# The adapter of a four-layer kernel: each batch's own columns by transfer, narrow fp32 products and one stacked product

## The reference, cut to what matters

```
x = x + L0(x)   # 64x64 weight chosen per batch (200 of them)
x = x + L1(x)   # attention over a paged cache, window 256, 8 heads, new keys and values written to the pages
x = x + L2(x)   # expert: x @ W[id] + b[id], 16 experts of 512x512
x = x + L3(x)   # x @ W.T + scalings[a] * ((x @ A[a].T) @ Bm[a].T), a = adapter number of the batch
```

## Time and profile before

| | us |
|---|---|
| median of 3 runs | 1035.92 |
| lowest and highest | 1035.61, 1037.2 |
| the profiled execution | 1039.95 |
| its span, first to last instruction | 1038.1 |
| PE busy in the span | 999.5 (96%) |
| DVE busy | 660.5 (64%) |
| POOL busy | 542.8 (52%) |
| ACT busy | 537.7 (52%) |

### The profile page before, as it was taken

The page is one execution under the profiler, slowest core; times in us unless marked ns, Lnnn a source line. Parts: engine busy times, 40 slices in busy tenths (PEclk is TensorE's granted clock), DMA queues, the critical chain, the costliest instruction groups (busy, mean ns, idle before and its releaser), DMA issues.

```text
span 1038.1 us, 24050 instructions
## 1 busy us (share of the span) xinstructions
PE 999.5 (96%) x6438; PEld 714.4 (69%) x6438; DVE 660.5 (64%) x1928; ACT 537.7 (52%) x1337; POOL 542.8 (52%) x597
## 2 busy tenths in 40 slices
PE   8998999999768999999999999999999999999998
PEld 6676777767635777766777766677766677777666
DVE  5897898666744656556656556655655665565562
ACT  4347776667444544455445455554545545544551
POOL 3553644446675555556555555656645555555500
PEclk9999999999969999999999999999999999999999
DMA  4333453365447767777677777767777776777650
GB/s 142 115 126 125 137 171 126 104 201 190 148 123 224 211 194 240 229 205 245 205 215 228 219 202 224 219 196 232 223 213 197 233 210 205 216 237 205 201 201 21
DMA packets 95338, 196.17 MB, mean 189 GB/s; under 512 B 31346, under 2 KB 40114, under 8 KB 87110
## 3 DMA queue, kind: packets, MB, share of 16 engines
q1 hardware_dynamic: 63942, 149.49, 45.8%
q0 software_dynamic: 30784, 44.16, 15.5%
q10 hardware_dynamic: 576, 2.10, 0.6%
HBM read 195.08 MB, written 33.56 MB: 220 GB/s over the span
## 4 chain that ended last, share of the span: by engine, by line
PE 68%; issue 1%; POOL 1%; DMA 1%; DVE 0%; ACT 0%; POOLq 0%; SPq 0%; DVEq 0%; ACTq 0%
PE bank L93 15%; PE bank L1506 12%; PE bank L1460 9%; PE bank L1481 9%; PE bank L1468 8%; PE bank L1556 6%; PE bank L1436 4%; PE bank L1447 3%; PE bank L1560 3%; DMA W<-in_w 1%; POOL KV L1152 0%; DMA KVE<-in_pool,idxs_e 0%; POOL KVE L1162 0%; POOL KV L1162 0%; PE bank L1527 0%
## 5 line engine op out<-in xcount | busy, mean ns | idle before, releaser
L1266 ACT ACTIVATE PR<-SM,nb 128x336 f32<-128x336 f32 x256 | 147.5, 585 | 6.5 <-DVE nb L1338 6.3
L1162 POOL DMA_INDIRECT KV<-kv_scratch,idxs x96 | 96.6, 1007 | 101.0 <-DMA KV<-in_pool,idxs 77.0
L1162 POOL DMA_INDIRECT KVE<-kv_scratch,idxs_e x93 | 93.4, 1004 | 95.6 <-DMA KVE<-in_pool,idxs_e 71.0
L1257 ACT ACTIVATE PT<-bank 112x384 f32<-112x384 f32 x256 | 111.4, 489 | 56.1 <-PE bank L1468 55.1
L1506 PE MATMUL bank<-W,XT 128*64 128x512 f32 x512 | 126.2, 609 | 3.7 <-DMA W<-in_w 3.7
L1152 POOL DMA_INDIRECT KV<-in_pool,idxs x96 | 98.8, 1029 | 49.2 <-issue 24.8
L1152 POOL DMA_INDIRECT KVE<-in_pool,idxs_e x90 | 92.9, 1032 | 54.5 <-issue 30.0
L93 PE MATMUL bank<-wqh,XTH 128*128 128x512 f32 x256 | 106.5, 416 | 9.0 <-DVE XTL L506 6.0
L1468 PE MATMUL bank<-ident,PR 128*112 128x128 f32 x768 | 108.8, 278 | 2.6 <-DVE PR L1345 2.6
L1468 PEld LDWEIGHTS bank<-ident,PR 128*112 128x112 f32 x768 | 83.5, 134 | 34.4 <-DVE PR L1345 19.8
L93 PE MATMUL bank<-wql,XTH 128*128 128x512 f32 x256 | 101.8, 398 | 0.0
(11 more groups left out here) (204 smaller groups left out, 2338.0 us busy)
## 6 DMA issues: line engine op xcount, KB each, us to landing
W<-in_w SPq DMA_DIRECT2D x64, 1024.0 KB, 5.6
X<-in_x SPq DMA_DIRECT2D x32, 256.0 KB, 2.9
x_scratch<-X SPq DMA_DIRECT2D x32, 256.0 KB, 2.0
qt_scratch<-QT SPq DMA_DIRECT2D x32, 256.0 KB, 2.9
XB<-x_scratch SPq DMA_DIRECT2D x32, 256.0 KB
BB<-in_b SPq DMA_DIRECT2D x64, 128.0 KB
out_dram<-XO SPq DMA_DIRECT2D x32, 256.0 KB
kv_scratch<-KVR SPq DMA_DIRECT2D x31, 256.0 KB, 3.1
```

The lines of the kernel that those rows point to most:

```text
L1162: pool.indirect_dma_start(out=KV[k][:, c, :], out_offset=None, in_=kv_d, in_offset=bass.IndirectOffsetOnAxis(ap=idxs[k][:, NCH + c:NCH + c ...
L1257: return nc.scalar.activation(dst, src, ACT.Copy)
L1266: nc.scalar.activation(PR[u % 2][:, :], SM[u % 2][:, :], ACT.Exp, bias=nb[:, u:u + 1], scale=SCALE, accum_out=rs[:, u:u + 1]).then_inc(s_e, 1)
```

## The change

The adapter no longer multiplies by all 8 adapters and masks. SP fetches for each batch its own part by its number:

- `AS` (SBUF, made in the first stage by ACT) holds each adapter's columns of A four times over, so 4 x 16 = 64 columns per 128 features. Two DMAs a pair copy 128 KB each from `AS` to `AG`.
- `bs_scratch` (DRAM, stored in the first stage by 4 DMAs, 1 MB in all) holds for each adapter 64 rows: high, high, low, low part of the scaled B. Two DMAs a pair copy 64 rows of 512 each (128 KB) to `BG`.
- `adapter` is 8 fp32 products (16 PE instructions): stationary 128 x 64 of `AG`, moving 64 columns of x3 turned, the two batches in the two column halves of the array, into 64 columns of bank 7.
- DVE makes from it `XA`, two 64 x 64 blocks on a diagonal whose rows are high, low, high, low part, and `adapted_sum` is one fp32r pass of 512 columns, `XA` by `BG`.
- ACT now copies the turned x3 whole to `XT3` (fp32). DVE makes both `XTH3` (a copy) and `XTL3` from it, in the place where `XTL3` was made.
- On PE `adapted_sum` stands in the middle of `output`, after two of its four column groups; `adapter` waits for the whole x3 and the A transfers, `dense3_low` for the low part.
- SP issues the four transfers between the store and `weights(1)`.
- In the first stage the late weights are four parts, not five; added are the scaling of B on DVE, two copies on ACT (2048 and 512 columns), a subtraction of 512 columns on DVE and the store of B.

```diff
+        bs_d = nc.dram_tensor("bs_scratch", [NA, 4, RANK, D], F32).ap()
...
+            BSH, BSL = (trig[:, :, :, :].rearrange("p a b c -> p (a b c)")[:, i * D:(i + 1) * D].bitcast(F32R)
+                        for i in range(2))
...
                 def late_low(i):
                     def run():
-                        dve.wait_ge(s_wlh, i + 1)
+                        dve.wait_ge(s_wlh, i + 1 + i // 2)
                         part = slice(i * 1024, (i + 1) * 1024)
                         split(wlh[:, part], wll[:, part], wlr[:, part]).then_inc(s_wl, 1)
                     return run
+
+                def scale_b():
+                    dve.wait_ge(s_wlate, 16 * 6)
+                    v.tensor_scalar(b_raw, b_raw, scal[:, 0:1], None, ALU.mult).then_inc(s_bsc, 1)
+
+                def adapter_low():
+                    dve.wait_ge(s_wlh, 3)
+                    split(BSH, BSL, b_raw).then_inc(s_wl, 1)
...
-                between.update({27: late_low(0), 28: late_low(1), 29: late_low(2),
-                                31: in_turn(late_low(3), late_low(4))})
+                between.update({21: go_on(1), 23: go_on(2), 26: in_turn(go_on(4), scale_b)})
+                between.update({27: late_low(0), 28: late_low(1), 29: adapter_low, 30: late_low(2), 31: late_low(3)})
...
+                def store_b():
+                    sp.wait_ge(s_wl, 3)
+                    for g in range(4):
+                        sp.dma_start(bs_d[:, g], (BSH, BSL)[g // 2].bitcast(F32)).then_inc(s_bso, 16)
...
+                    30: store_b,
...
+                def adapter_high():
+                    act.wait_ge(s_bsc, 1)
+                    copy(AS[:, :, :, :], a_raw.rearrange("p (e r) -> p e r", r=RANK).unsqueeze(2).to_broadcast(
+                        [P, NA * KC, 4, RANK]))
+                    copy(BSH, b_raw).then_inc(s_wlh, 1)
...
+                       {26: in_turn(late_high(0), late_high(1)), 27: adapter_high, 28: late_high(2), 29: late_high(3)})
...
+                    def adapter_columns(q):
+                        numbers = [sp.value_load(aid[0:1, bass.ds(q * 2 + b, 1)], min_val=0, max_val=NA - 1)
+                                   for b in range(2)]
+                        wait(sp, s_xa, q)
+                        for b, e in enumerate(numbers):
+                            sp.dma_start(AG[:, b, :], AS[:, :, :, :].rearrange("p (e k) s r -> p e (k s r)", e=NA)
+                                         [:, bass.ds(e, 1)].rearrange("p o c -> p (o c)")).then_inc(s_ag, 16)
+                        wait(sp, s_l3, q)
+                        for b, e in enumerate(numbers):
+                            sp.dma_start(BG[b * T:(b + 1) * T, :].bitcast(F32), bs_d[bass.ds(e, 1)]
+                                         .rearrange("o g r n -> (o g r) n")).then_inc(s_bg, 16)
...
                         store(pr.move(-2))
+                    if dense:
+                        adapter_columns(p - 1)
...
-                        copy(XTH3[:, :, :].rearrange("p k t -> p (k t)"), bank[7][:, :]).then_inc(s_xt3h, 1)
+                        copy(XT3[:, :, :].rearrange("p k t -> p (k t)"), bank[7][:, :]).then_inc(s_xt3f, 1)
...
+                        dve.wait_ge(s_xt3f, at(r, 1, 0))
+                        wait(dve, s_l3, r)
+                        v.tensor_copy(XTH3[:, :, :], XT3[:, :, :]).then_inc(s_xt3h, 1)
                         dve.wait_ge(s_xt3h, at(r, 1, 0))
-                        low(XTL3[:, :, :].rearrange("p k t -> p (k t)"), bank[7][:, :],
-                            XTH3[:, :, :].rearrange("p k t -> p (k t)")).then_inc(s_xt3, 1)
+                        low(XTL3[:, :, :], XT3[:, :, :], XTH3[:, :, :]).then_inc(s_xt3, 1)
...
-                        v.tensor_tensor(XAM[:, :, :], bank[1 if last_dense(p) else 7][:, 0:P].rearrange("p (b t) -> p b t", b=2),
-                                        adapt[:, bass.ds(r * 2, 2)].unsqueeze(2).to_broadcast([P, 2, T]),
-                                        ALU.mult).then_inc(s_xam, 1)
-                        xam = XAM[:, :, :].rearrange("p b t -> p (b t)")
+                        xa = bank[1 if last_dense(p) else 7][:, 0:T]
+                        v.tensor_copy(XAH[:, :], xa).then_inc(s_xah, 1)
+                        v.tensor_scalar(XAM[:, :], xa, sel[:, 1:2], None, ALU.mult).then_inc(s_xam, 1)
+                        dve.wait_ge(s_xah, at(r, 1, 0))
                         dve.wait_ge(s_xam, at(r, 1, 0))
-                        v.tensor_copy(XAH[:, :], xam).then_inc(s_xah, 1)
-                        dve.wait_ge(s_xah, at(r, 1, 0))
-                        low(XAL[:, :], xam, XAH[:, :]).then_inc(s_xal, 1)
+                        wait(dve, s_l3, r)
+                        for b in range(2):
+                            rows = slice(b * T, (b + 1) * T)
+                            v.scalar_tensor_tensor(XA[rows, rows], XAH[rows, :].bitcast(F32), sel[rows, 0:1],
+                                                   XAM[rows, :], ALU.mult, ALU.add).then_inc(s_xal, 1)
...
                 def adapter(r, of):
-                    pe.wait_ge(s_xt3, at(r, 1, 0))
-                    exact_products(mm, bank[of][:, 0:P], [(a_h[:, k, :], a_l[:, k, :], *x3t[k]) for k in range(KC)],
-                                   True, True).then_inc(s_xa, 1)
+                    pe.wait_ge(s_xt3f, at(r, 1, 0))
+                    pe.wait_ge(s_ag, at(r, 32, 31))
+                    for k in range(KC):
+                        for b in range(2):
+                            rows = slice(b * T, (b + 1) * T)
+                            last = mm(bank[of][rows, 0:T], AG[:, b, k * T:(k + 1) * T], XT3[:, k, rows],
+                                      start=k == 0, stop=k == KC - 1, skip_group_check=True)
+                    last.then_inc(s_xa, 1)
 
                 def adapted_sum(r, of):
-                    pe.wait_ge(s_xal, at(r, 1, 0))
-                    exact_products(mm, bank[of][:, :], [(XAH[:, :], XAL[:, :], b_h[:, 0, :], b_l[:, 0, :])],
-                                   False, True).then_inc(s_l3, 1)
+                    pe.wait_ge(s_xal, at(r, 2, 1))
+                    pe.wait_ge(s_bg, at(r, 32, 31))
+                    mm(bank[of][:, :], XA[:, :], BG[:, :], start=False, stop=True).then_inc(s_l3, 1)
...
-                def dense3_low():
+                def dense3_low(r):
+                    pe.wait_ge(s_xt3, at(r, 1, 0))
                     for k in range(KC):
                         mm(bank[6][:, :], XTL3[:, k, :], w3_h[:, k, :], start=False, stop=False)
...
-                        dense3_low()
+                        dense3_low(r)
+                    if dense:
+                        if adapted:
+                            pe.wait_ge(s_xah, at(r, 1, 0))
+                            pe.wait_ge(s_xam, at(r, 1, 0))
+                        output(q, 0, 2)
+                    if adapted:
                         adapted_sum(r, 6)
                     if dense:
-                        if adapted:
-                            pe.wait_ge(s_xam, at(r, 1, 0))
-                        output(q, 0, KC)
+                        output(q, 2, KC)
                     if attention:
```

More of the change, by code:

```diff
@@ L129, in build @@
         eid = sb("eid", [1, NB], I32)
[L130 removed]
+        aid = sb("aid", [1, NB], I32)
+        sel = sb("sel", [P, 2])
         KVE = sb("KVE", [CH, 2 * NCH * KVW])
@@ L137, in build @@
         FM_e = [early[:, D + i * SPAN:D + (i + 1) * SPAN] for i in range(2)]
-        NWL = KC * D * 2 + KC * P + D
+        NWL = KC * D * 2
+        NWR = NWL + KC * P + D
         wlh = sb("wlh", [P, NWL], F32R)
         wll = sb("wll", [P, NWL], F32R)
+        AS = sb("AS", [P, NA * KC, 4, RANK])
         def late(tile, which):
-            a, n = {"wo": (0, D), "w3": (KC * D, D), "a": (2 * KC * D, P), "b": (2 * KC * D + KC * P, D)}[which]
-            k = 1 if which == "b" else KC
-            return tile[:, a:a + k * n].rearrange("p (k n) -> p k n", k=k)
+            a = {"wo": 0, "w3": KC * D}[which]
+            return tile[:, a:a + KC * D].rearrange("p (k n) -> p k n", k=KC)
         s_const = sem("const_ready")
@@ L173, in build @@
         s_wl = sem("late_split")
+        s_bsc = sem("b_scaled")
+        s_bso = sem("b_stored")
         s_xth = sem("x1t_high")
@@ L211, in sa @@
                 return pa.enter_context(nc.sbuf_tensor(name, shape, dt))
-            wlr = sa("wlr", [P, NWL])
+            wlr = sa("wlr", [P, NWR])
+            a_raw = wlr[:, NWL:NWL + KC * P]
+            b_raw = wlr[:, NWL + KC * P:NWR]
             wqkv = wlr[:, 0:KC * 1024].rearrange("p (k n) -> p k n", k=KC)
@@ L484, in indices @@
                     yield
-                    step(v.tensor_scalar(pns[:, :], pni[:, :], 4, None, ALU.arith_shift_right))
+                    step(v.tensor_scalar(pns[:, :], pni[:, :], 4, 1, ALU.arith_shift_right, ALU.bitwise_and))
                     yield
@@ L489, in indices @@
                     yield
```

(23 more changed lines are left out.)

15 lines of the change are left out of this document (7 added, 8 removed).

## The result

The changed kernel takes 1088.93 us, the median of 4 runs (1083.62 to 1092.73), against 1036.56 (1035.61 to 1040.33) for the kernel before: ratio 1.0494, 95% interval [1.0442, 1.0547]. It is slower by 52 us where 9 less were forecast, and outside the range. The profiled execution took 1087.78 us, with a span of 1086.0; before it was 1038.1.

A forecast was written before the change was run, and what follows sets the result against it. PE was taken as the bound, end to end over a pair of 22.53 us. Pairs -6.3, ends -2.2, boundary -0.6 and early A +0.5 gave -8.6 us: median 1027.3, range 1018 to 1042.

The forecast's parts named there:

- What leaves PE: On PE, adapter with values shrinks by 0.65 us and the stacked product by 0.46: 1.11 us a pair.
- rivals 1 and 3: Narrow adapter products on PE: at 0.055 us each, 1035.0 us (chance 0.18); at 0.075, 1045 us (chance 0.07).
- the values behind would speed up: On PE, the values behind the new adapter in column halves would take 0.66 us instead of 0.81.
- The stacked product: `adapted_sum` on PE as one pass in place of three: 0.46 us a pair leave.
- What enters before `dense3_high`: PE waits there for DVE's copy to `XTH3`, 0.42 us long: 0.90 us a pair, bounds 0.75 and 1.16.
- rival 2: POOL's gathers hold up DVE's copy, middle price 0.5 us a pair: 1042 us, chance 0.10.
- Rival 6: The wait before `dense3_high` does not show because DVE comes earlier: 1000 us, chance 0.03.
- Ends and boundary: Bodies 32 and 33 gain 2.2 us together; the boundary after the last pair gains 0.6, bounds 0 and 1.2.
- an early A: In the first bodies the transfers have a shorter lead: 0.5 us booked once, bounds 0 and 5.
- Transfers: Four DMAs a pair, 0.5 MB, hidden in the middle; POOL could take 2.2 us more in every other pair: nothing.
- Rival 5: Fuller DMA makes the gathers the bound and the pair stays at 22.5 us: about 1034 us, chance 0.07.
- rival 4: A lands late for PE, 1 us in each pair: 1057 us, chance 0.05.

The follow-up runs named there:

- g2: Changed kernel with the four transfers made for the first pair only, later pairs reusing that A and B: 1032.41 us, ratio 0.9958 to the kernel before.
- g4: Changed kernel with the four transfers issued ahead of `weights(0)` and x3's high part made by ACT again: 1047.68 us, ratio 1.0119 to the kernel before.
- g1: Changed kernel with the four transfers issued ahead of `weights(0)`: 1049.46 us, ratio 1.0126 to the kernel before.
- g3: Changed kernel with each pair's transfers in the late place but into unread tiles, products using A and B fetched once: 1082.55 us, ratio 1.0441.
- h3: g2 with each pair's two number loads kept in SP's list: 1132.71 us, in a job where the kernel before took 1120.66.
- i2: Changed kernel without per-pair transfers, ACT copying A and B by number and making x3's high part: 1114.14 us, kernel before 1125.53 there.
- f1: Changed kernel with the four transfers issued ahead of `weights(0)`: 1113.78 us, in a job where the kernel before took 1161.79.
- h1: Kernel before plus two number loads and the four transfers per pair into unread tiles: 1097.21 us, kernel before 1120.66 there.

## Why the prediction was wrong, step by step

**What leaves PE: right.** The timeline of PE's loads before, and then in g2:

```profile
720.77 0.35 PEld L1447 LDWEIGHTS bank<-ident,KV 112*128 112x128 f32 x3
...
722.59 0.19 PEld L1556 LDWEIGHTS bank<-wll,XTH 128*128 128x128 f32 x1
...
725.23 0.30 PEld L1460 LDWEIGHTS bank<-KT,QB 64*128 64x128 f32 x4 [0.17 <-issue]
```

```profile
704.23 0.19 PEld L1579 LDWEIGHTS bank<-BG,XA 128*128 128x128 f32 x1
704.47 0.19 PEld L93 LDWEIGHTS bank<-wlh,OTH 128*128 128x128 f32 x1
...
717.98 0.35 PEld L1499 LDWEIGHTS bank<-ident,KV 112*128 112x128 f32 x3
719.19 0.19 PEld L1614 LDWEIGHTS bank<-wlh,XTH 128*128 128x128 f32 x1 [0.87 <-DVE XTH L1421]
...
720.70 0.19 PEld L1614 LDWEIGHTS bank<-wll,XTH 128*128 128x128 f32 x1
721.25 0.55 PEld L1572 LDWEIGHTS bank<-XT,AG 128*64 128x64 f32 x16 [0.37 <-issue]
721.71 0.64 PEld L1533 LDWEIGHTS bank<-PT,KVE 112*64 112x64 f32 x12
722.52 0.30 PEld L1512 LDWEIGHTS bank<-KT,QB 64*128 64x128 f32 x4 [0.17 <-issue]
```

From the last load of `dense3_high` to the scores' first load it was 725.23 - 722.59 = 2.64 us before and is 722.52 - 720.70 = 1.82 now: 0.82 leave for 0.65 forecast, and so in each of the 27 pairs from 400 to 1000 us. The sixteen narrow instructions start 0.029 us apart (0.46 / 16), near the floor of 0.0275, so rivals 1 and 3 fall. The first of them comes 0.55 us behind the last load of `dense3_high` (720.70 to 721.25); the old adapter's came 0.23 behind. That the values behind would speed up did not hold (0.81 as before), which the adapter's pace makes good: the sum was nearly right with two terms off against each other. The Trainium skill (TensorE: Matmul & The Clock Gate, LDWEIGHTS) would have 53 ns for each load of 64 columns; in two column halves they did not add up in series. The halves take turns, so each has a load every 0.058 us, which agrees. The stacked product takes 0.24 for 0.70 (three loads 0.23 apart): 0.46, as forecast.

**What enters before `dense3_high`: right in place and kind, too small by 0.2.** The start of L1614 lies 1.21 us behind that of L1499's transposes; before, L1556's (721.08) lay 0.31 behind L1447's: 0.90. That is the least: in every other pair it is 0.3 more (the copy starts later on DVE), and over 400 to 1000 us the mean is 1.08 us more than before, for 0.90 forecast. So the 1.28 that leave and the 1.08 that enter are both 0.2 above the forecast's 1.11 and 0.90, and that their difference comes out near is in part luck. Most of g2's pairs alternate between 22.17 and 22.47, mean of all 22.41, for 22.32 forecast. In the changed kernel the same wait stands (701.65 to 702.13), and the copy takes (the line's view, then one case):

```profile
L1421 DVE CAST XTH<-XT x32: 417/427/642, 336.8 to 1077.8; 128x512 fp32r<-128x512 f32 x32
```

```profile
701.65 0.43 DVE L1421 CAST XTH<-XT 128x512 fp32r<-128x512 f32 x1
...
702.13 0.19 PEld L1614 LDWEIGHTS bank<-wlh,XTH 128*128 128x128 f32 x1 [0.87 <-DVE XTH L1421]
```

427 ns in the middle, 642 at most, for 0.42 forecast. No copy was held for a gather's 1 us, so rival 2 falls by its size. It is not nothing: six of the 32 copies took 0.47 to 0.64 us, each with a gather under way, like the one at 724.16 (0.63 us) beside the gather at 723.58 shown above; together 0.7 us in the whole run. Other copies of the same kernel were as short as ever inside a gather's record (383.37, 0.43 us, in the gather from 383.00 to 383.99). So the rule of the exclusive lock (the Trainium skill, SBUF: State Buffer, "SBUF: two separate sides") is borne out only in part, with no full gather of waiting. That the copy in its turn holds up gathers can't be the loss either, since g2 has the same 32 copies. Rival 6 falls by the same wait.

**Ends and boundary: right.** g2's span of 1030.7 is 7.4 below before: pairs 4.1 (forecast 6.1 for 29), start 0.6 (0.6), the last body and the end 2.75 (2.2). The forecast without its 0.5 for an early A is 9.1 for this. By the medians of one job it is only 4.9, since the profiled execution of before was 4.0 above the median; so the work on PE gave half to four fifths of what was forecast for it.

**Transfers: wrong, and the whole of the miss.** Two sentences failed. "8 to 8.5. That is hidden": behind the two number loads A is issued 2.75 us after `weights(0)` (720.97 - 718.22), not directly, and `weights(0)` itself comes later when the gathers do, as it waits for them. And the one that carries the loss: "POOL could take that much more before it set the pace: nothing." The slack was read rightly as far as it went (KVE's 24.5 us; KV has 23.5 more, and both are 1.8 us a pair), but its user was not sized. By POOL's clock over 400 to 1000 us, divided by the number of pairs in them (600 over the mean distance):

| kernel | mean pair | landing waits | waits for PE | the rest |
|---|---|---|---|---|
| before | 22.55 | 4.7 | 1.8 | 16.0 |
| g2, no transfers | 22.41 | 5.7 | 0.9 | 15.8 |
| g4, early, ACT high | 22.70 | 7.0 | 0 | 15.7 |
| g1, early | 23.00 | 7.3 | 0 | 15.7 |
| g3, late, unread | 24.14 | 8.7 | 0 | 15.5 |
| after | 24.25 | 8.8 | 0 | 15.5 |

The rest is the twelve gathers at 1.3 us each, which no run shortened. So POOL's loop is 15.5 to 16 us plus the landings, and before it had 1.8 us left. From before to after, the landing waits grew by 4.1 us. Less the slack that is 2.3, and less the 0.5 by which the rest is smaller, it is, but for rounding, the 1.7 by which a pair grew. This is bookkeeping; what the transfers did is g3 against g2, which differ by them and by what SP does for them (number loads and waits): landing waits 3.0 longer, 0.9 of that taken from the waits for PE and 0.3 from the rest, and a pair of 24.14 for 22.41, 1.73 more or 50 us in 29 pairs. (The other 1.0 of the 4.1 is in g2 too.) The trace of before had a place to see it, though it is not in the rows above the prediction: the half in which the four transfers go out was the one with the quick landing, 2.1 us; A and B are issued beside its gathers. The error was to ask only whether A is in time, and not what A delays. Rival 5 named the mechanism, with a chance of 0.07, but kept the pair at 22.5, as if the gathers could only use up the gain; rival 4 had the price, by a wait that g3 shows not to be the cause.

**Still open.** How much of the 3.0 is bytes and how much SP's time: h3 was made for that, and its condition spoiled it. For bytes speak two things. SP itself idles for landed gathers for 283.6 us in the changed kernel between 290 and 1050 us, so its 1.8 us for numbers are mostly covered. And in the code POOL's gathers wait for PE, for POOL's own copies and for landings, never for SP, so SP's time can lengthen POOL's loop only through when its transfers meet the gathers. That is argued, not shown by a run. Why the same bytes cost 33 us more in the late place than in the early one: the table has it as landings, 8.7 for 7.3 us a pair, but which transfer stood in front of which gather there was not separated. And whether the adapter without transfers beats the kernel before with the selection made: g2 shows that the products alone do, by 4.9 us, and i2's shortest pair was 21.44 us, but no undisturbed run of a complete version that beats it exists.

## What to carry to other kernels

A transfer that is in time can still cost its kernel more than all it saves: price it by what is issued beside and behind it on the DMA engines, and look for the loop that waits for landings, here 15.5 us of gather issues plus two landings in a pair of 22.5. Slack read as a wait on another engine is a budget; set against it a bound on the delay, from the shortest landing that the new transfer touches, and not "nothing". A wait for a landing can itself hide slack, as in g2, so compare two runs that differ by the transfer alone. When a new wait in the trace is as large as the loss, take it away and leave its transfers, before calling it the cause.

## What the runs showed of the hardware that was not expected

Narrow fp32 products of 64 by 64 in the two column halves start 0.029 us apart, 16 in 0.46 us. The landing of 128 KB from SBUF to SBUF took 5.8 us (median, g3, 400 to 1000 us) among W and the gathers, as long as W's megabyte in the kernel before (5.6). VectorE's fp32 copy from SBUF to SBUF is sometimes stretched beside a gather that GpSimd is issuing, by 0.22 us at most and in six of 32 cases. And a job can have a condition in which engines start instructions up to 12 us late (the longest "remote" wait, in f1: 12.1) and the kernel before takes 1119 to 1162 us: there kernels with more transfers were not slower, and h1 was 1.1% below before (ratio 0.9889 [0.9780, 0.9998], an interval that all but reaches 1); why is not known.
